# Post-norm transformer layer: transposing the softmax numerators with DMA in float16 halves, in a new order of work

## The chip, the cores and the metric

One core of one Trainium2 chip runs the whole layer in one launch. The metric is the device time of that launch in microseconds (us). The kernel before takes 672.68 us, the median of three runs (672.47 to 676.06).

## The reference

Four independent sequences of T=512 tokens with D=512 features go through one layer. All inputs and outputs are float32.

```python
q = (x @ Wq + bq)                 # 16 heads of 32
k = (x @ Wk + bk); v = (x @ Wv + bv)      # one key/value head shared by all 16
q, k = rotary(q), rotary(k)
attn = softmax(q k^T / sqrt(32))          # per head 512 x 512
x = layernorm(x + (attn v) @ Wo + bo)
quant(w) = clip(round(w / (mean|w| + 1e-8)), -1, 1)
hidden = sigmoid(x @ quant(w1)^T) * (x @ quant(w2)^T)    # 1408 wide
x = layernorm(x + hidden @ quant(w3)^T)
```

## The kernel before, in words

Five engines work at once, each from its own queue in order: TensorE (PE) multiplies, VectorE (DVE) and ScalarE (ACT) do elementwise work, GpSimd (POOL) helps and issues DMAs, SyncE (SP) issues DMAs. Order across engines is kept by counting semaphores: `wait_ge(sem, n)` in a queue blocks everything behind it in that queue until the count is reached.

**Periods.** `period(0)` does the attention of sequence 0 (`first_heads`) while the weights are loaded and rounded to -1, 0, 1. `period(b)`, b = 1 to 3, does the attention of sequence b, and beside it everything that comes after attention for sequence b-1: output projection (`project_out`), layer norm, transposing the normalised rows (`turn_h`), the up projections (`up`, two per tile f: one for the gate, one for the value), `down`. A tail does the rest of sequence 3.

**A head** is four score tiles of 128 queries x 512 keys (`score`, L1017). For each tile DVE takes the row maximum (`row_max`, L756), ACT the exponential with its row sum (`exps`, L526; an ACTIVATE and a READ_ACCUMULATOR) into p_sb. PE then transposes p in 128x128 blocks (`turn`, L1028), 16 a head, into two PSUM banks t_ps; ACT (`move`, L534) and DVE (`move`, L763) copy two of the four banks of a head each to pt_sb. After four heads `context` (L1084) multiplies pt_sb with v in float32: 16 products of 32 columns, four of them side by side in the array. `turn_sums`, `norm_row` and `normalise` divide by the row sums.

**What sets the order.** Each engine has a written order (`heads` for PE at L1138, ACT at L574, DVE at L812). BESIDE (L51) names the one late job that stands beside each head: head 0 to 3 up0 to up3, head 4 projection q2, and so on: at most one up tile a head. Between two periods stands a stage without heads (L1185 to L1202): q0, k, v, four output projections, four `turn_h`, q1. The score tiles go round three banks s_ps (four in sequence 0). a_ps and b_ps are filled by one job at a time; `up` fills a_ps with the gate and b_ps with the value; ACT takes tanh of a_ps (L509), DVE multiplies (`gate`, L707), ACT rounds the product to float16 (`g_high`, L518), DVE takes the remainder (`g_low`, L712). In ACT's order the `g_high` that is owed from the head before stands ahead of the exponentials.

**q** is rotated, split in two parts (hi, lo) and stacked for the scores by 16 DMAs of 64 KB per group of four heads (`stack`, L310): group 0 by SP, groups 1 to 3 by POOL. The rotation's cosine product is POOL's (L393), the sine product and the sum DVE's (L658, L667), in sequence 0 POOL's.

Of the kernel before, what the change touches and what calls it, by code (L numbers as in the profile page):

```python
# [20 lines left out]
F32 = mybir.dt.float32  # L22
F32R = mybir.dt.float32r
F16 = mybir.dt.float16
ALU = mybir.AluOpType
# [3 lines left out]
P = 128  # L29
# [6 lines left out]
FT = F // P  # L36
SCALE = float(HD) ** -0.5
# [4 lines left out]
G_SCALE = 2 * H_SCALE  # L42
PTR = HPG
QR = 2
SUMS = 4
PIECES = 4
SR = 3
# [3 lines left out]
BESIDE = (["up0", "up1", "up2", "up3", "q2", "up4", "up5", "up6", "q3"]  # L51
          + [f"up{f}" for f in range(7, FT)] + ["dn0", "dn1", "dn2", "dn3"])
FIRST_Q_AT = [3, 7]
DOWN_FIRST = 4
DOWN_CUT = 7


# [6 lines left out]
TAIL = [f"{stage}{t}" for stage in ("wo", "ht") for t in range(TT)]  # L64
LAST_CUT = 6


def is_tail(period):

    return isinstance(period, int) and period == B  # L70


def is_last(period):
    return isinstance(period, int) and period == B - 1


def norm_count(c, ln, t):


    n = (c * 2 + ln) * TT + t  # L80
    if isinstance(c, int) and (c, ln, t) == (B - 2, 1, TT - 1):
        n += TT
    elif isinstance(c, int) and (c, ln) == (B - 1, 0):
        n -= 1
    return n + 1


def late_bank(period, use):

    return "a" if use in ("wo0", "wo2", "wo3") else "b"  # L90


def bank_uses(bank, period):


    first = isinstance(period, int) and period == 0
    last = is_tail(period)
    uses = []
    if not last:
        uses += ["q0"] if bank == "a" else ["k"]  # L100
    if not first and not last:
        uses += [use for use in [f"{stage}{t}" for stage in ("wo", "ht") for t in range(TT)]
                 if late_bank(period, use) == bank]
    if not last and bank == "a":
        uses += ["q1"]
    for h in range(H + 1):
        use = BESIDE[h]
        if use[:1] == "q" and bank == "a" and not last:
            uses.append(use)
        elif use[:2] == "up" and not first:  # L110
            uses.append(use)
        elif use[:2] == "dn" and not first and (int(use[2:]) % 2 == 0) == (bank == "a"):
            uses.append(use)
        if h % HPG == 0 and h and bank == "a" and not last:
            uses.append(f"r{h // HPG - 1}")
    return uses


def at_use(bank, period, use):

    count = bank_uses(bank, period).index(use) + 1
    if isinstance(period, int) and period == 0:
        return count
    return len(bank_uses(bank, 0)) + (period - 1) * len(bank_uses(bank, None)) + count


def layer(nc, xT, x, wq, small, wo, b_rows, w1, w2, w3, table, out):
    with ExitStack() as ctx:
# [5 lines left out]

# [62 lines left out]

# [24 lines left out]
        b_drained = sem("b_drained")  # L222
        kv_filled = sem("kv_filled")
# [7 lines left out]
        q_in = [sem(f"q_in{j}") for j in range(HPG)]  # L231
        q_by_pool = [sem(f"q_by_pool{j}") for j in range(HPG)]
# [5 lines left out]
        pt_dve = sem("pt_dve")  # L238
        recip_done = sem("recip_done")
# [21 lines left out]

        def ain(b, use):

            return at_use("a", b, use)

        def bin_(b, use):
            return at_use("b", b, use)

        def wide(n):

            return (a_ps, a_filled, a_drained, ain) if n % 2 == 0 else (b_ps, b_filled, b_drained, bin_)

        def late_tile(b, use):

            if is_tail(b):
                ps = (s_ps + t_ps + [c_ps] + s_ps)[TAIL.index(use)]
                return ps, tail_filled, tail_drained, lambda b, use: TAIL.index(use) + 1
            return wide(0) if late_bank(b, use) == "a" else wide(1)

        def score_ring(b):  # L280

            return SR + 1 if isinstance(b, int) and b == 0 else SR

        def score_bank(b, n):
            return (s_ps + [b_ps])[n % score_ring(b)][:, :]

        def gated_tile(b, f):


            return raw[:, f % 2, :] if is_tail(b) else b_ps[:, :]  # L290

        def stacked(b, g, j):

            if isinstance(b, int) and b == 0:
                return q_in[j], (g + 1) * 16 * 4
            if g == 0:
                return q_in[j], (b + HG) * 16 * 4
            return q_by_pool[j], ((b - 1) * (HG - 1) + g) * 16 * 4

        def stack(engine, b, g):  # L300

            engine.wait_ge(hi_done, b * len(UNITS) + UNITS.index(f"q{g}") + 1)
            stand(engine)
            for j in range(HPG):
                for r in (0, 2, 1, 3):
                    half = (hi, lo)[r % 2]
                    if j == 0 and r == 1:
                        engine.wait_ge(lo_done, b * len(UNITS) + UNITS.index(f"q{g}") + 1)
                        stand(engine)
                    engine.dma_start(q_st[HD * r:HD * (r + 1), g % QR * HPG + j, :].bitcast(F32),  # L310
                                     half[HD * j:HD * (j + 1), :].bitcast(F32)).then_inc(stacked(b, g, j)[0], 16)
# [7 lines left out]


        @block.sync
        def _(sp):
            def load_xT(b):
                for half in range(2):
                    cols = slice(half * DT * T // 2, (half + 1) * DT * T // 2)
                    sp.dma_start(xT_sb[:, :, :].rearrange("p k t -> p (k t)")[:, cols],
                                 xT[b, :, cols]).then_inc(xT_in[half], 16)

            def store(c, t):
                sp.wait_ge(normed, norm_count(c, 1, t))  # L330
                stand(sp)
                sp.dma_start(out[c, t * P:(t + 1) * P, :], h_sb[:, t, :]).then_inc(h_free, 16)

            def period(b):
                first, last = isinstance(b, int) and b == 0, isinstance(b, int) and b == B - 1
                if first:
                    sp.wait_ge(xT_in[1], 16)
                    sp.dma_start(wq_sb[:, :, P:], wq[:, P:].rearrange("(k p) n -> p k n", p=P)).then_inc(wq_in, 16)
# [938 lines left out]
```

## Time and profile before

| | |
|---|---|
| median of three runs | 672.68 us |
| the profiled execution: its own time | 671.8 us |
| its span, first to last instruction | 670.0 us |
| granted TensorE clock, mean over the span | 0.983 |
| PE busy | 627.5 us (94%) |
| DVE busy | 458.3 us (68%) |
| ACT busy | 353.3 us (53%) |
| POOL busy | 202.1 us (30%) |

A busy share is the union of the engine's instructions. The durations of single instructions overlap their neighbours on the same engine a little, so a train of them takes less than the sum: the distance from one start to the next is what one costs the engine, its duration is what a dependent has to wait.

### The profile page before, as it was taken

Reading aid. Unit: us, or ns where it says so; the run is one execution under the profiler, and the core shown is the slowest. Engines: PE = TensorE matmul, PEld = TensorE weight load, DVE = VectorE, ACT = ScalarE, POOL = GpSimd, SP = SyncE. Lnnn points to the kernel's source line nnn. Section 1 sums busy time; section 2 is a strip of 40 time slices with the busy share of each in tenths; the row PEclk is TensorE's granted clock in tenths of the full one; section 3 lists DMA queues with packets and bytes.
Section 4 is the critical chain, followed back from the end, with each engine's and each line's share of the span. In section 5 each row is a group of like instructions: output and inputs, shape, how many; then the busy total and the mean of one; then the engine's idle time right before and its main releaser. Section 6 shows DMA issues by size and latency. Waiting matters only on the chain.

```text
span 670.0 us, 10715 instructions
## 1 busy us (share of the span) xinstructions
PE 627.5 (94%) x3342; PEld 340.9 (51%) x3342; DVE 458.3 (68%) x791; ACT 353.3 (53%) x814; POOL 202.1 (30%) x292
## 2 busy tenths in 40 slices
PE   5777968899999999999999999999999999999996
PEld 2544554345556556435656565534556564543442
DVE  2776777387878776577877785577878785655333
ACT  2787696316767675114867674313767675302320
POOL 1229689221450700121440610122422340110001
PEclk9699979999999999999999999999999999999999
DMA  7661532021221200022210400022201110000001
GB/s 275 216 232 32 204 94 98 0 64 64 64 64 55 73 1 1 35 84 75 65 44 21 127 1 1 33 79 80 63 21 44 32 33 0 28 22 16 1 1 63
DMA packets 18204, 41.93 MB, mean 63 GB/s; under 512 B 4704, under 2 KB 5856, under 8 KB 17632
## 3 DMA queue, kind: packets, MB, share of 16 engines
q1 hardware_dynamic: 12576, 30.42, 13.7%
q0 software_dynamic: 4608, 9.45, 5.8%
q10 hardware_dynamic: 960, 1.33, 0.5%
q8 instruction: 30, 0.49, 0.3%
q14 instruction: 30, 0.25, 0.1%
HBM read 20.20 MB, written 4.19 MB: 36 GB/s over the span
## 4 chain that ended last, share of the span: by engine, by line
PE 81%; DVE 5%; ACT 5%; issue 3%; DMA 3%; SPq 1%; POOL 0%; DVEq 0%; POOLq 0%; ACTq 0%
PE t_ps L1028 15%; PE b_ps L988 11%; PE a_ps L988 11%; PE c_ps L1084 9%; PE a_ps L942 8%; PE s_ps L1017 7%; PE a_ps L1003 6%; PE b_ps L1003 5%; PE a_ps L966 5%; DMA late<-in_w 2%; PE b_ps L966 2%; ACT p_sb L526 2%; SPq L310 1%; ACT pt_sb L534 1%; DVE sh_sb L756 1%
## 5 line engine op out<-in xcount | busy, mean ns | idle before, releaser
L526 ACT ACTIVATE p_sb<-s_ps,sh_sb 128x512 f32<-128x512 f32 x240 | 164.4, 689 | 87.1 <-DVE sh_sb L756 87.0
L756 DVE TENSOR_REDUCE sh_sb<-s_ps 128x1 f32<-128x512 f32 x240 | 157.9, 681 | 4.3 <-PE s_ps L1017 4.3
L1028 PE MATMUL t_ps<-table_sb,p_sb 128*128 128x128 f32 x1024 | 140.7, 280 | 13.4 <-ACT pt_sb L534 10.9
L1028 PEld LDWEIGHTS t_ps<-table_sb,p_sb 128*128 128x128 f32 x1024 | 120.2, 144 | 58.4 <-ACT p_sb L526 23.1
L763 DVE COPY pt_sb<-t_ps 128x512 f32<-128x512 f32 x128 | 88.3, 690 | 85.0 <-PE t_ps L1028 83.6
L534 ACT ACTIVATE pt_sb<-t_ps 128x512 f32<-128x512 f32 x128 | 76.5, 598 | 54.7 <-PE t_ps L1028 53.1
L1017 PE MATMUL s_ps<-k_st,q_st 128*128 128x512 f32 x240 | 89.9, 457 | 3.8 <-DVE k_st L676 2.0
L988 PE MATMUL b_ps<-late,q 128*128 128x512 f16 x352 | 83.5, 380 | 0.0
L988 PE MATMUL a_ps<-late,q 128*128 128x512 f16 x344 | 81.6, 380 | 2.0 <-DVE late L692 2.0
L417 POOL TENSOR_SCALAR rstd<-mv 128x1 f32<-128x1 f32 x32 | 8.5, 265 | 236.3 <-DVE mv L719 236.2
L393 POOL TENSOR_TENSOR rot<-raw,table_sb 128x512 f32<-128x512 f32 x20 | 25.4, 1272 | 154.7 <-ACT raw L493 139.3
L942 PE MATMUL a_ps<-xT_sb,wq_sb 128*128 128x512 f32 x128 | 62.3, 618 | 7.9 <-DMA wq_sb<-in_wq 6.8
L1084 PE MATMUL c_ps<-pt_sb,v_sb 128*32 128x512 f32 x512 | 60.5, 597 | 3.1 <-ACT pt_sb L534 3.1
L310 POOL DMA_DIRECT2D q_st<-hi x72 | 36.1, 506 | 59.2 <-DVE hi L683 51.8
L988 PEld LDWEIGHTS a_ps<-late,q 128*128 128x128 f16 x344 | 31.0, 98 | 43.5 <-issue 6.6
L988 PEld LDWEIGHTS b_ps<-late,q 128*128 128x128 f16 x352 | 31.8, 98 | 39.1 <-issue 5.3
L1017 PEld LDWEIGHTS s_ps<-k_st,q_st 128*128 128x128 f32 x240 | 42.3, 196 | 15.3 <-ACT p_sb L526 7.6
L526 ACT ACTIVATION_READ_ACCUMULATOR p_sb<-s_ps,sh_sb 128x1 f32 x240 | 48.2, 201 | 0.0
L1003 PE MATMUL b_ps<-q,late 128*128 128x512 f16 x176 | 41.3, 379 | 0.0
L1003 PE MATMUL a_ps<-q,late 128*128 128x512 f16 x176 | 40.4, 380 | 0.0
L942 PEld LDWEIGHTS a_ps<-xT_sb,wq_sb 128*128 128x128 f32 x128 | 23.6, 197 | 31.0 <-issue 20.7
L707 DVE SCALAR_TENSOR_TENSOR b_ps<-th,b_ps 128x512 f32<-128x512 f32 x33 | 23.0, 696 | 21.4 <-PE b_ps L988 19.1
(97 smaller groups left out, 679.1 us busy)
## 6 DMA issues: line engine op xcount, KB each, us to landing
late<-in_w SPq DMA_DIRECT2D x2, 2816.0 KB, 11.4
q_st<-hi POOLq DMA_DIRECT2D x72, 64.0 KB, 2.0
q_st<-lo POOLq DMA_DIRECT2D x72, 64.0 KB, 2.0
xT_sb<-in_xT SPq DMA_DIRECT2D x8, 512.0 KB, 4.7
late<-in_x SPq DMA_DIRECT2D x4, 1024.0 KB, 5.3
out<-late SPq DMA_DIRECT2D x16, 256.0 KB, 2.0
q_st<-hi SPq DMA_DIRECT2D x56, 64.0 KB, 2.0
q_st<-lo SPq DMA_DIRECT2D x56, 64.0 KB, 2.0
```

Source lines behind the costliest of these rows:

```text
L310: engine.dma_start(q_st[HD * r:HD * (r + 1), g % QR * HPG + j, :].bitcast(F32), half[HD * j:HD * (j + 1), :].bitcast(F32)).then_inc(stacke ...
L526: act.activation(p_sb[:, h % 2, t, :], score_bank(b, n), ACT.Exp, bias=sh_sb[:, n % (2 * SR):n % (2 * SR) + 1], scale=-1.0, accum_out=sums ...
L534: act.activation(pt_sb[:, h % PTR, k, :], t_ps[k % 2][:, :], ACT.Copy).then_inc(pt_act, 1)
L756: dve.tensor_reduce(sh_sb[:, n % (2 * SR):n % (2 * SR) + 1], score_bank(b, n), AX.X, ALU.min).then_inc(maxed, 1)
L763: dve.tensor_copy(pt_sb[:, h % PTR, k, :], t_ps[k % 2][:, :]).then_inc(pt_dve, 1)
L942: mm = pe.matmul(a_ps[:, :], wq_sb[:, k, g * P:(g + 1) * P], xT_sb[:, k, :], start=(k == 0), stop=(k == DT - 1))
L966: mm = pe.matmul(ps[:, :], cx[:, g, t * P:(t + 1) * P], wo_sb[:, g, :], start=(g == 0), stop=(g == HG - 1))
L988: mm = pe.matmul(ps[:, :], w[:, k, f * P:(f + 1) * P], hT[:, s, k, :], start=(k == 0 and s == 0), stop=(k == DT - 1 and s == 1))
L1003: mm = pe.matmul(ps[:, :], gT[:, s, f, t * P:(t + 1) * P], q3v[:, f, :], start=(f == 0 and s == 0), stop=(f == FT - 1 and s == 1))
L1017: pe.matmul(score_bank(b, n), q_st[:, h % (QR * HPG), t * P:(t + 1) * P], k_st[:, :], start=True, stop=True).then_inc(scored, 1)
L1028: mm = pe.transpose(t_ps[k % 2][:, t * P:(t + 1) * P], p_sb[:, h % 2, t, k * P:(k + 1) * P], id_sb)
L1084: mm = pe.matmul(c_ps[HD * j:HD * (j + 1), :], v_sb[:, k, :], pt_sb[:, (g * HPG + j) % PTR, k, :], start=(k == 0), stop=(k == TT - 1))
```

## The change

Sequence 0 stays nearly as it was. From sequence 1 on:

- Scores, maxima and buffers go by pairs of tiles: four PSUM banks hold two pairs, one maximum instruction reads a pair. The second transpose bank is now e_ps, a third bank for other jobs.
- p of a pair is scaled by 4096 and split: ACT writes the float16 rounding (`p_high`), DVE the float16 remainder (`p_low`). SP issues one DMA transpose of both halves, 512 KB, into pt_sb (`turn`), two a head. PE's 256 transposes a sequence and the 64 copies of `move` are gone.
- `context` multiplies both halves of p with both halves of v (v is scaled by a power of two and split, `values`, `value_halves`): 64 float16 products instead of 16 in float32, and it waits for the eight transposes of its group.
- There is no stage without heads: all jobs stand in BESIDE beside the 32 half heads, up to two up tiles a head in heads 6, 7, 10 and 11. The context of a group stands at the second head after it.
- All stacking is POOL's, head by head, and so is the rest of the rotation of q1 to q3 in every sequence. Loops over b are written out.

```diff
+BESIDE = [                       # (after the head's 1st pair of scores), (after its 2nd pair)
+    ([("dn2", -2)], []),
+    ([("sums3", -1), ("ctx3", -1)], [("dn3", -2)]),
+    ([("vp", 0), ("wo0", -1)], [("wo1", -1)]),
+    ([("wo2", -1)], [("wo3", -1), ("vs", 0)]),
+    ([("q2", 0)], [("vb", 0), ("ht0", -1), ("ht1", -1)]),
+    ([("ht2", -1), ("ht3", -1), ("ctx0", 0), ("sums0", 0)], [("up0", -1)]),
+    ([("up1", -1)], [("up2", -1)]),
+    ([("up3", -1)], [("up4", -1)]),
+    ([("q3", 0)], [("up5", -1)]),
+    ([("ctx1", 0), ("sums1", 0)], [("up6", -1)]),
+    ([("up7", -1)], [("up8", -1)]),
+    ([("up9", -1)], [("up10", -1)]),
+    ([("dn0", -1)], []),
+    ([("ctx2", 0), ("sums2", 0)], [("q0", 1)]),
+    ([("dn1", -1)], [("kp", 1)]),
+    ([("ks", 1)], [("q1", 1)]),
+]
+# PE
+            def heads(b):
+                for h in range(H):
+                    for half in range(2):
+                        score(b, h, half)
+                        for name, s in beside(b, h, half):
+                            use(name, s)
+            def score(b, h, i):
+                n = h * PAIRS + i
+                pe.wait_ge(expd, b * H * TT + max(2 * n - 2, 0))
...
+            def context(b, g):
+                pe.wait_ge(ctx_done, b * HG + g)
+                pe.wait_ge(v_lo, b)
+                for n in range(PSLOTS):
+                    pe.wait_ge(turned[n], ...)
+                for k in range(TT):
+                    for n in range(2):
+                        for m in range(2):
+                            for j in range(HPG):
+                                mm = pe.matmul(c_ps[HD * j:HD * (j + 1), :], vh[:, m, k, :],
+                                               pt_half[:, j, :, n, :, k, :], ...)
+# SP
+            def turn(b, h, i):
+                n = pair_of(b, h, i) % PSLOTS
+                sp.wait_ge(p_lo, pair_of(b, h, i) + 1)
+                sp.wait_ge(ctx_filled, b * HG + h // HPG)
+                sp.dma_start_transpose(pt_half[...], p_half[n][...]).then_inc(turned[n], 16)
+# ACT
+            def heads(b):
+                    exps(b, h, 0)
+                    exps(b, h, 1)
+                    if owed:
+                        g_high(owed[1], owed[0])
+                    for f, s in early:
+                        tanh(s, f)
+                    if h == 5:
+                        h_high(b - 1, 2)
+                        h_high(b - 1, 3)
+                    p_high(b, h, 0)
+                    for f, s in early:
+                        g_high(s, f)
...
+                    exps(b, h, 2)
+                    exps(b, h, 3)
...
+                    if h == 8:
+                        unit(b, "q3")
+                    if h % HPG == 1 and h > HPG:
+                        norm_row(b, h // HPG - 1)
+                    for f, s in late_ups:
+                        tanh(s, f)
+                        owed = f, s
+                    p_high(b, h, 1)
...
+# DVE
+            def heads(b):
+                    row_max(b, h, 0)
+                    if owed is not None:
+                        g_low(s, owed)
+                    if h:
+                        p_low(b, h - 1, 1)
...
+                    for f in early:
+                        gate(s, f)
+                    row_max(b, h, 1)
+                    for f in early:
+                        g_low(s, f)
+                    p_low(b, h, 0)
+                    if h == 5:
+                        h_low(s, 2)
+                        h_low(s, 3)
+                    for f in late_ups:
+                        gate(s, f)
+                        owed = f
...
```

`early` are the up tiles of the head's first half, `late_ups` those of its second. On DVE the output projections' sums, norms and `ffn_out` (the residual after `down`) stand between `p_low(b, h-1, 1)` and the early `gate`, or at the end of the head; in head 5 `norm(3)`, `h_low(0)` and `h_low(1)` stand ahead of the second maximum. A job waits until its bank's job before has been read: `ht0` and `ht2` share b_ps, `q3` and `up5` a_ps, `sums1` and `up6` a_ps, `dn2` and `sums3` a_ps.

## Rows read from the trace of the kernel before

**Rows 1.** Windows: sequence 0, periods 1 to 3, tail; PE, PEld, DVE, ACT, POOL busy, clock, DMA
```profile
0.00:128.70 128.70, 97.06 (x529) 56.78 (x529) 82.79 (x141) 85.92 (x197) 70.59 (x57) 0.92 0.44 150
128.70:282.50 153.80, 152.56 (x834) 83.51 (x834) 112.31 (x194) 83.90 (x197) 41.02 (x71) 1.00 0.17 46
436.00:587.10 151.10, 149.96 (x826) 82.44 (x824) 113.19 (x196) 83.92 (x197) 41.81 (x73) 1.00 0.16 43
587.10:670.00 82.90, 75.43 (x326) 34.38 (x322) 37.10 (x64) 15.66 (x26) 7.28 (x18) 0.99 0.05 19
```

**Rows 2.** The page's chain that ended last, by engine
```profile
PE 81%; DVE 5%; ACT 5%; issue 3%; DMA 3%; SPq 1%; POOL 0%; DVEq 0%; POOLq 0%; ACTq 0%
```

**Rows 3.** Groups by line and shape: count, busy us, mean ns of one, idle before
```profile
L1028 PE MATMUL t_ps<-table_sb,p_sb 128*128 128x128 f32 x1024 | 140.7, 280 | 13.4 <-ACT pt_sb L534 10.9 <-ACT p_sb L526 1.8
L763 DVE COPY pt_sb<-t_ps 128x512 f32<-128x512 f32 x128 | 88.3, 690 | 85.0 <-PE t_ps L1028 83.6
L534 ACT ACTIVATE pt_sb<-t_ps 128x512 f32<-128x512 f32 x128 | 76.5, 598 | 54.7 <-PE t_ps L1028 53.1
L756 DVE TENSOR_REDUCE sh_sb<-s_ps 128x1 f32<-128x512 f32 x240 | 157.9, 681 | 4.3 <-PE s_ps L1017 4.3
L724 DVE TENSOR_SCALAR late<-late,mv,rstd 128x512 f32<-128x512 f32 x32 | 17.2, 536 | 9.1 <-POOL rstd L420 9.0
L543 ACT ACTIVATE q<-late 128x1408 f16<-128x1408 f32 x12 | 16.5, 1383 | 1.5 <-DMA late<-in_w 1.3
L1057 PE MATMUL c_ps<-table_sb,rexp 128*128 128x32 f32 x32 | 3.9, 266 | 0.0
```

**Rows 4.** Timeline of PE, period 1: context, then one head with an up tile (start, us)
```profile
189.52 3.64 PE L1084 MATMUL c_ps<-pt_sb,v_sb 128*32 128x512 f32 x32
196.79 0.94 PE L1017 MATMUL s_ps<-k_st,q_st 128*128 128x512 f32 x3
197.57 1.90 PE L988 MATMUL a_ps<-late,q 128*128 128x512 f16 x8
199.31 1.04 PE L1028 MATMUL t_ps<-table_sb,p_sb 128*128 128x128 f32 x8
202.96 0.94 PE L1017 MATMUL s_ps<-k_st,q_st 128*128 128x512 f32 x3
```

**Rows 5.** Timeline of DVE and ACT in that head
```profile
198.87 1.28 DVE L756 TENSOR_REDUCE sh_sb<-s_ps 128x1 f32<-128x512 f32 x2
199.59 0.69 ACT L526 ACTIVATE p_sb<-s_ps,sh_sb 128x512 f32<-128x512 f32 x1 [0.42 <-DVE sh_sb L756]
200.27 0.68 ACT L526 ACTIVATE p_sb<-s_ps,sh_sb 128x512 f32<-128x512 f32 x1
200.93 0.59 ACT L534 ACTIVATE pt_sb<-t_ps 128x512 f32<-128x512 f32 x1
201.41 0.60 ACT L509 ACTIVATE th<-a_ps 128x512 f32<-128x512 f32 x1
```

**Rows 6.** Timeline of heads of sequence 0 that have no other work beside them
```profile
113.16 1.16 PE L1028 MATMUL t_ps<-table_sb,p_sb 128*128 128x128 f32 x8 [0.34 <-ACT pt_sb L534]
...
117.88 1.16 PE L1028 MATMUL t_ps<-table_sb,p_sb 128*128 128x128 f32 x8 [0.34 <-ACT pt_sb L534]
```

**Rows 7.** DMA issues (KB each, median us to landing)
```profile
late<-in_w SPq DMA_DIRECT2D x2, 2816.0 KB, 11.4
q_st<-lo POOLq DMA_DIRECT2D x72, 64.0 KB, 2.0
```

**Rows 8.** Windows of sequence 0 at the lower clock (columns as in the first group)
```profile
24.00:28.00 4.00, 4.00 (x12) 2.50 (x11) 2.28 (x5) 4.00 (x9) 2.55 (x2) 0.50 0.59 133
88.00:92.00 4.00, 2.45 (x10) 2.38 (x11) 2.74 (x5) 4.00 (x13) 3.83 (x4) 0.50 0.33 80
```

More of the change, by code:

```diff
@@ L42 @@
 G_SCALE = 2 * H_SCALE
+P_SCALE = 2.0 ** 12
+V_TOP = 14
+EXPONENT = 0x7F800000
 PTR = HPG
-QR = 2
+PSLOTS = 4
+QR = 5
 SUMS = 4
 PIECES = 4
-SR = 3
+FIRST_RING = 4
 UNITS = ["q0", "k", "q1", "q2", "q3"]
[L51 to L55, printed above, removed]
+FIRST_Q_AT = [3, 7, 15]
+FIRST_Q = [(0, 2), (0, 3), (1, 0)]
 ABS_AT = [0, 0, 1, 1, 2, 3, 4, 5, 9, 9, 10, 10]
@@ L61 @@
 ROUND = 1.5 * 2.0 ** 23
[L64 to L90, printed above, removed]
@@ L93, in bank_uses @@
[L93 to L116, printed above, removed]
@@ new lines, with beside @@
+LAST_BESIDE = {13: ([("ctx2", 0), ("sums2", 0)], [("dn1", -1)]), 14: ([("dn2", -1)], []), 15: ([], [])}
+TAIL = ([("dn3", B - 2), ("sums3", B - 1)] + [(f"ht{t}", B - 1) for t in range(TT)]
+        + [(f"up{f}", B - 1) for f in range(FT)] + [(f"dn{t}", B - 1) for t in range(TT)])
+def beside(b, h, half):
+    uses = BESIDE[h][half]
+    if b == B - 1 and h in LAST_BESIDE:
+        uses = LAST_BESIDE[h][half]
+    return [(use, b + of) for use, of in uses if not (use[:2] == "dn" and b + of < 0)
+            and not (b == 1 and (use, of) in (("sums3", -1), ("ctx3", -1)))]
@@ L284, in score_bank @@
[L284 to L311, printed above, removed]
+        wide = {"a": (a_ps, a_filled, a_drained), "b": (b_ps, b_filled, b_drained),
+                "e": (e_ps, e_filled, e_drained)}
@@ L375, in _ @@
+            turn(B - 1, H - 1, 1)
+            for t in range(1, TT):
+                store(B - 2, t)
             for t in range(TT):
                 store(B - 1, t)
-            sp.wait_ge(h_free, (B + 1) * TT * 16)
+            for t in range(TT):
+                sp.wait_ge(h_free[t], (B + 1) * 16)
         @block.gpsimd
@@ L910, in _ @@
+            first_heads()
+            rotate(1, "q0")
+            halves(1, "q0")
+            normalise(0, HG - 1)
+            pairs(1, "k")
+            rotate(1, "k")
+            halves(1, "k")
+            for b in range(1, B):
+                heads(b)
+            p_low(B - 1, H - 1, 1)
+            reciprocals(B - 1, HG - 1)
+            norm(B - 2, 1, 2)
+            ffn_out(B - 2, 3)
+            norm(B - 2, 1, 3)
+            normalise(B - 1, HG - 1)
             for t in range(TT):
+                attended(B - 1, t)
```

1367 lines of the change are left out of this document (730 added, 637 removed).

## The prediction, made before the changed kernel was built or run

> **What bounds the kernel now.** I read the windows first: in the three periods PE is busy 152.6 of 153.8 us and 150.0 of 151.1, DVE about 113, ACT 84 [rows 1]. The chain of waits agrees: 81% of it is PE [rows 2]. So a microsecond taken from PE in a period is a microsecond off the kernel, but only until another engine, or the order of the queues, stops it. The bound is near: DVE has 40 us of room a period. Sequence 0 (128.7 us) is different: PE is busy 97 us there, and what sets its pace is the ring score, maximum, exponential, transpose.
>
> **What PE loses and gains.** From one head's scores to the next are 202.96 - 196.79 = 6.17 us; eight float16 products take 199.31 - 197.57 = 1.74 us, 0.2175 each [rows 4]. Sixteen of them (3.48) and the scores (0.94) leave 1.75 us for 16 transposes, 28 us a sequence. The context is the term that the trace does not show. Now it is 32 instructions in 3.64 us, four column groups side by side, so 8 rounds of 0.45 [rows 4]. The float16 one is 64 products, 16 rounds. Lower end: 16 x 0.2175 = 3.5 us. Upper end: each pair of weight load and product costs what the small products of L1057 cost, 3.9 / 32 = 0.12 us [rows 3], 64 x 0.12 = 7.7. I take 3.6, because the context's own row is the nearest and it does overlap. PE's work per sequence then falls from 152.5 to about 124.5 us.
>
> **What ACT and DVE lose and gain.** I distinguish the distance between starts (what an instruction costs its engine) from its duration (what the next engine waits). On ACT exponentials start 0.67 us apart, a copy costs 0.48; on DVE two maxima take 1.28, so one costs 0.60 and lasts 0.68 [rows 5].
> - ACT drops 32 copies a sequence (15 us) and gets 32 `p_high` of 1024 columns. From 598 ns at 512 columns and 1383 at 1408 [rows 3] another 512 columns are 0.45 us: 0.93 each, 29 us. ACT: 84 to 98 us.
> - DVE drops 32 copies (19 us). A maximum over a pair is 0.60 + 0.53 = 1.13 us (a 512-column pass is 0.536 [rows 3]), 32 x 1.13 = 36 for 64 x 0.60 = 38. `p_low` reads two operands of 1024 columns: by the same sum 1.13, 36 us a sequence. Bounds: half of that if the wide form runs faster (18), and 1.30 each when POOL's work slows it. Rotation moved to POOL gives back 4, the bound and halves of v cost 1.5. DVE: 113 to about 125 us.
> - POOL gets 16 more stacking DMAs and six more rotation products a sequence, some 53 us of work in a period; SP has 32 transposes to issue, and `load_x` waits behind the turn of head 5, `add_bias` behind that, two stacks behind `add_bias`. In the timetable below none of them is waited for, since q is stacked two to four heads ahead. They cost nothing as long as heads last over 8 us.
>
> If only these sums counted, the change would pay: see the first rival. But every engine works strictly in its written order, and the new order puts dependent work on three engines into one ring.
>
> **The ring of a head with two up tiles** (heads 6, 7, 10, 11). Pass a semaphore in 0.05 us, and start when DVE begins the first maximum: maximum 1.30; two exponentials on ACT 1.34 (0.67 each); the owed `g_high`, which now stands behind them, 0.67; DVE, which has stood at `g_low` all that time, does it in 0.60; `p_low` of the head before 1.13; early `gate` 0.60; second maximum 1.30; two exponentials 1.34; late tanh 0.67; late `gate` 0.60; next head. Sum 9.55 us. PE has only 0.94 + 4 x 1.74 = 7.9 us to do in it, so PE waits. Before, the same two tiles stood beside two heads of 6.17.
>
> **The other heads** I carried through in the same way: each instruction starts when the one before it in its queue has left the engine and all that it waits for is done. The method can be tried on sequence 0, where a ring and not PE sets the pace: it gives 4.69 us for a plain head, and the trace has 117.88 - 113.16 = 4.72 [rows 6]. For sequence 2, heads 0 to 15, it gives
> 13.3, 13.0, 9.2, 8.3, 10.8, 18.7, 9.5, 9.6, 14.2, 14.4, 9.6, 9.6, 11.8, 12.2, 10.6, 12.7: 187 us, where the period now takes 153.5. The long ones are these.
> - Head 0: `dn2` (22 x 0.2175 = 4.8 us) stands on PE ahead of the second pair of scores; DVE idles 6.9 us for it. Head 1: `sums3` waits until DVE has read `dn2`'s bank, then the context (3.6) stands ahead of the second scores.
> - Head 5: `ht2` waits for `h_low(0)` of the same bank, which stands behind a maximum, `p_low` and a norm; then the context; the second scores come 5.1 us late. Then `up0` waits for `h_low(3)`, and `gate` for `up0`: 3.9 us.
> - Heads 8 and 9: `up5` needs a_ps, which holds q3 until ACT reads it behind the second exponentials; DVE stands at `gate` meanwhile, 4.8 us. Head 9 is the same with the row sums (`norm_row`).
> - Head 15 and the next 0: k of the next sequence is rotated and split only when its scores are next.
>
> **The sum.** Sequence 0 to the first maximum of sequence 1: 128.7 [rows 1] and about ten dependent steps of 0.7 for k (its product, bias, rotation, halves, score), 136 us. Sequence 1 has no late `dn`, `sums3` and `ctx3` in heads 0 and 1: 170. Sequence 2: 187. Sequence 3, whose last heads have little beside them, to its last exponential: 177. Tail on PE from there: output projections and `dn3` not yet done 12, context 3.6, last group 3.4; then 6.5 for sum, statistics, norm, transpose, halves; up 11 x 3.48 = 38.3; down 4 x 4.79 = 19.2; last norm and store 6: 89 (now 82.9 [rows 1]). Together 136 + 534 + 89 = 759 us of span. The profiled execution is 1.8 us above its span now and the median 0.9 above that: **762 us**, 13% slower. (A difference under 0.5% could not be told from none here.)
>
> **Transfers.** The trace has no transpose by DMA. Lower end: the large weight loads move 2816 KB in 11.4 us [rows 7], so 512 KB in 2.1. Upper end: eight times a small transfer of 64 KB, issue to landing 2.0 [rows 7], 16 us. I take 3, plus 2 to land, since a 512 KB transfer is nearest to the large loads. In the timetable nothing changes up to 4.5 us per transfer; 5 gives 554 in place of 534, 6 gives 626, 8 gives 810.
> The Trainium skill's VectorE: DVE Perf Modes, section The three transpose paths, prices a 128x128 transpose in 2-byte numbers at 1309 ns by DMA; a transfer here has 16 such blocks, which would be an estimated 21 us, far slower than TensorE. Its DMA: Bandwidth & Descriptors, section Latency and other measured facts, has 261 GB/s for such transposes, an estimated 2.0 us a transfer, which by the timetable would be hidden. No row here decides between them.
>
> **The clock.** Where PE worked with gaps in sequence 0 the granted clock fell to 0.50, the lower level of 1.2 GHz, for instance in 88 to 92 with PE busy 2.45 of 4 us [rows 8]; in the periods it is 1.00 [rows 1]. After the change PE is busy some 65% of a period. If the mean were 0.92 as in sequence 0, PE's 124.5 us would grow by 11 a sequence, partly on the ring: bounds 0 and +33, taken as 0, since mostly PE is what waits.
>
> **Rivals.**
> 1. The queues overlap better than the timetable has it, and the fullest engine sets the pace: DVE's 125 us a sequence. 136 + 375 + 89 + 2.7 = 603 us. For it: PE is at 99% now, its order is loose enough. Against: the ring of 9.55 us is dependent work, and sequence 0, also a ring, has no engine above 76% [rows 1]. It decides if heads 6 and 7 last under 7.9 us. This is the other side. 0.13.
> 2. The ring holds, but the long heads do not: all 16 heads take about 9.6. 136 + 3 x 153 + 89 + 2.7 = 687 us. 0.10.
> 3. The DMA transposes bound it: every transfer above 4.5 us is waited for by the exponentials (four buffers) and the contexts. At 6 us each 762 + 92 = 854 us, at 8 us 1038; at the upper end of 16 us the 96 transfers alone would take 1536, the whole 1764. For it: no row shows such a transfer. Against: nothing but the rate of the large loads. 0.15. (The 1309 ns of the skill's page VectorE: DVE Perf Modes would put it beyond that upper end.)
> 4. As forecast, 0.62. Its own range: `p_low` at half -25, context at 7.7 us +37, DVE at 1.30 +9, clock up to +33: 735 to 815.
>
> **Range and chances.** The range takes in rival 2 and rival 3 up to 6 us: 685 to 860; outside remain rival 1 and the slow half of rival 3, about 0.2. Faster by over 0.5%: rival 1 and a sliver of 2, 0.14. Within 0.5% lies none of the cases, 0.02. Slower: 0.84.
>
> **What would show it.** In the profile after, heads 6, 7, 10, 11 start 9.6 us apart and head 5 is the longest; DVE's `g_low` begins after an idle 2 us that ended with ACT's `g_high`; `gate` in heads 8 and 9 after more than 4; PE is busy under 75% in a sequence with a mean clock below 0.98; the contexts last 3.6 us and don't end on a DMA wait; `p_low` starts 1.13 before the next instruction. I am wrong if PE or DVE is above 90% busy in a sequence, or if exponentials idle on transfers.

## The result and the profile after

The changed kernel takes **829.68 us** (median), the kernel before 672.93 beside it: a ratio of 1.227, 95% interval 1.217 to 1.238. One of its four executions took 1060.36 us at a clock of 0.55 and is left out of the comparison. The forecast of 762 had the sign right and was 68 us short. The time lies in the whole range, 685 to 860, but above the 735 to 815 that the forecast gave its own case: the part of the range that it fell into had been allowed for slow transfers, which did not happen.

The page of the changed kernel: span, busy time by engine, the granted clock in 40 slices, the chain that ended last, and the main groups.

```profile
span 827.4 us, 9098 instructions
PE 608.9 (74%) x2964; PEld 288.1 (35%) x2964; DVE 510.7 (62%) x698; ACT 394.4 (48%) x814; POOL 256.4 (31%) x358
PEclk9899898969889886897988989679888898987998
PE 41%; DVE 28%; ACT 12%; issue 12%; DMA 4%; SPq 2%; POOL 0%; DVEq 0%; ACTq 0%; POOLq 0%
L621 ACT ACTIVATE p_all<-s_ps,sh_sb 128x512 f32<-128x512 f32 x192 | 130.0, 682 | 240.2 <-DVE sh_sb L883 240.1
L883 DVE TENSOR_REDUCE sh_sb<-s_ps 128x2 f32<-128x1024 f32 x96 | 116.8, 1218 | 93.2 <-PE s_ps L1201 93.2
L890 DVE SCALAR_TENSOR_TENSOR p_all<-p_all 128x1024 f16<-128x1024 f32 x96 | 131.6, 1371 | 3.6 <-ACT p_all L629 3.5
L629 ACT ACTIVATE p_all<-p_all 128x1024 f16<-128x1024 f32 x96 | 101.7, 1059 | 1.4
L1253 PE MATMUL c_ps<-pt_sb,vh 128*32 128x512 f16 x768 | 59.3, 478 | 11.9 <-DMA pt_sb<-p_all 11.9
```

No engine is full. PE was 81% of the chain [rows 2] and is 41% now; maxima, exponentials and scores wait for each other (L621 for L883, L883 for L1201). The window of sequence 2, then the waits of DVE and PE (us, times, longest):

```profile
323.60:531.80 208.20, 146.49 (x708) 66.44 (x708) 131.04 (x166) 97.66 (x197) 59.56 (x96) 0.84 0.61 117
```
```profile
DVE late L842 <- ACT late L600: 49.3, 32, 2.0
DVE b_ps L837 <- PE b_ps L1163: 47.1, 12, 6.1
DVE e_ps L837 <- PE e_ps L1163: 28.2, 8, 7.1
...
PE b_ps L1138 <- DVE late L828: 29.0, 3, 9.7
PE a_ps L1221 <- DVE late L860: 12.2, 2, 6.1
PE c_ps L1253 <- DMA pt_sb<-p_all: 11.9, 3, 4.0
PE s_ps L1201 <- DVE k_st L785: 10.8, 3, 4.8
```

A period of 151 to 154 us at clock 1.00 [rows 1] is now, in sequence 2, 208 at 0.84. Of the 32 waits of `g_low` for `g_high` (L842 for L600), 21 last 2.00 us, seven in each sequence from head 6 to head 12: they are the ring of the prediction. The other 11, of 0.66 us, are the tail's. The ring's length can be read from the maxima of heads 10 and 11 (DVE timeline; the first maximum of a head is the one behind the late `gate`):

```profile
462.95 1.22 DVE L883 TENSOR_REDUCE sh_sb<-s_ps 128x2 f32<-128x1024 f32 x1
...
472.40 1.22 DVE L883 TENSOR_REDUCE sh_sb<-s_ps 128x2 f32<-128x1024 f32 x1
...
481.85 1.22 DVE L883 TENSOR_REDUCE sh_sb<-s_ps 128x2 f32<-128x1024 f32 x1
```

9.45 us, twice; the prediction said 9.55. All heads of sequence 2, read in the same way (us from a head's first maximum to the next head's); the last line is of experiment e12 below:

| head | 0 | 1 | 2 | 3 | 4 | 5 | 6 | 7 | 8 | 9 | 10 | 11 | 12 | 13 | 14 | 15 | sum |
|---|---|---|---|---|---|---|---|---|---|---|---|---|---|---|---|---|---|
| forecast | 13.3 | 13.0 | 9.2 | 8.3 | 10.8 | 18.7 | 9.5 | 9.6 | 14.2 | 14.4 | 9.6 | 9.6 | 11.8 | 12.2 | 10.6 | 12.7 | 187 |
| measured | 15.3 | 15.1 | 9.4 | 8.3 | 12.6 | 23.4 | 13.8 | 9.4 | 16.3 | 15.6 | 9.4 | 9.5 | 7.9 | 17.9 | 10.7 | 13.5 | 208 |
| e12 | 13.4 | 13.3 | 9.4 | 8.3 | 12.6 | 20.6 | 9.4 | 9.4 | 13.9 | 17.1 | 9.9 | 9.5 | 7.9 | 15.5 | 10.7 | 13.4 | 194 |

**Where the 68 us lie.** First maximum of sequence 1 at 133.8 (forecast 136); the sequences take 189.8, 208.2 and 194.5 (170, 187, 177), the third up to the last exponential, and the tail after it 101.1 (89).

### The profile page after: what moved, and what is told of

It is laid out like the page before. It is cut to its first block, busy times and chain, and to the rows that moved or that the text cites. A ratio compares the mean times of both kernels' runs of the same rounds, so it can differ in the third digit from the quotient of the medians.

```text
span 827.4 us, 9098 instructions
## 1 busy us (share of the span) xinstructions
PE 608.9 (74%) x2964; PEld 288.1 (35%) x2964; DVE 510.7 (62%) x698; ACT 394.4 (48%) x814; POOL 256.4 (31%) x358
## 4 chain that ended last, share of the span: by engine, by line
PE 41%; DVE 28%; ACT 12%; issue 12%; DMA 4%; SPq 2%; POOL 0%; DVEq 0%; ACTq 0%; POOLq 0%
DVE sh_sb L883 10%; DVE p_all L890 8%; PE a_ps L1163 6%; PE c_ps L1253 6%; ACT p_all L621 5%; PE b_ps L1175 3%; PE a_ps L1175 3%; PE b_ps L1163 3%; PE a_ps L1094 2%; PE a_ps L1148 2%; PE s_ps L1201 2%; PE c_ps L1239 2%; PE e_ps L1163 2%; PE s_ps L1148 2%; PE b_ps L1148 2%
## 5 line engine op out<-in xcount | busy, mean ns | idle before, releaser
L621 ACT ACTIVATE p_all<-s_ps,sh_sb 128x512 f32<-128x512 f32 x192 | 130.0, 682 | 240.2 <-DVE sh_sb L883 240.1
L883 DVE TENSOR_REDUCE sh_sb<-s_ps 128x2 f32<-128x1024 f32 x96 | 116.8, 1218 | 93.2 <-PE s_ps L1201 93.2
L1163 PE MATMUL a_ps<-late,q 128*128 128x512 f16 x352 | 103.8, 448 | 71.9 <-ACT th L592 29.6
L890 DVE SCALAR_TENSOR_TENSOR p_all<-p_all 128x1024 f16<-128x1024 f32 x96 | 131.6, 1371 | 3.6 <-ACT p_all L629 3.5
L629 ACT ACTIVATE p_all<-p_all 128x1024 f16<-128x1024 f32 x96 | 101.7, 1059 | 1.4
L1201 PE MATMUL s_ps<-k_st,q_st 128*128 128x512 f32 x192 | 80.8, 509 | 19.2 <-DVE k_st L785 10.8
L461 POOL TENSOR_TENSOR rot<-raw,table_sb 128x512 f32<-128x512 f32 x20 | 25.8, 1290 | 144.0 <-ACT raw L571 136.2
L1253 PE MATMUL c_ps<-pt_sb,vh 128*32 128x512 f16 x768 | 59.3, 478 | 11.9 <-DMA pt_sb<-p_all 11.9
L1201 PEld LDWEIGHTS s_ps<-k_st,q_st 128*128 128x128 f32 x192 | 35.8, 198 | 43.6 <-issue 24.5
L837 DVE SCALAR_TENSOR_TENSOR b_ps<-th,b_ps 128x512 f32<-128x512 f32 x24 | 16.7, 696 | 51.2 <-PE b_ps L1163 47.1
L369 POOL DMA_DIRECT2D q_st<-lo x96 | 47.3, 497 | 0.0
L1163 PE MATMUL b_ps<-late,q 128*128 128x512 f16 x192 | 46.5, 386 | 0.0
L592 ACT ACTIVATE th<-a_ps 128x512 f32<-128x512 f32 x44 | 26.3, 598 | 41.3 <-PE a_ps L1163 41.3
L842 DVE TENSOR_TENSOR late<-b_ps,late 128x512 f16<-128x512 f32 x24 | 16.6, 692 | 40.0 <-ACT late L600 40.0
L608 ACT ACTIVATE p_all<-s_ps,sh_sb 128x512 f32<-128x512 f32 x48 | 32.9, 692 | 15.9 <-DVE sh_sb L877 15.9
L1163 PE MATMUL e_ps<-late,q 128*128 128x512 f16 x160 | 40.3, 397 | 0.0
```

Source lines behind the costliest of these rows:

```text
L369: engine.dma_start(q_st[HD * r:HD * (r + 1), slot, :].bitcast(F32), half[HD * (h % HPG):HD * (h % HPG + 1), :].bitcast(F32)).then_inc(stac ...
L608: act.activation(p_sb[:, h % 2, t, :], first_bank(n), ACT.Exp, bias=sh_sb[:, n % (2 * PSLOTS):n % (2 * PSLOTS) + 1], scale=-1.0, accum_out ...
L621: act.activation(p_pair[n][:, t % 2, :], pair_banks(h * PAIRS + t // 2)[:, t % 2, :], ACT.Exp, bias=sh_sb[:, 2 * n + t % 2:2 * n + t % 2 + ...
L629: act.activation(p_half[n][:, 0, :], p_pair[n].rearrange("p t k -> p (t k)"), ACT.Copy, scale=P_SCALE).then_inc(p_hi, 1)
L883: dve.tensor_reduce(sh_sb[:, 2 * n:2 * n + 2], pair_banks(h * PAIRS + i), AX.X, ALU.min).then_inc(maxed, 2)
L890: dve.scalar_tensor_tensor(out=p_half[n][:, 1, :], in0=p_pair[n].rearrange("p t k -> p (t k)"), scalar=P_SCALE, in1=p_half[n][:, 0, :], op ...
```

## What two timelines show

PE in head 5 of sequence 2:

```profile
377.55 0.70 PE L1201 MATMUL s_ps<-k_st,q_st 128*128 128x512 f32 x2
387.91 1.09 PE L1138 MATMUL b_ps<-table_sb,late 128*128 128x128 f32 x4 [9.66 <-DVE late L828]
388.79 1.06 PE L1138 MATMUL e_ps<-table_sb,late 128*128 128x128 f32 x4
389.79 5.56 PE L1253 MATMUL c_ps<-pt_sb,vh 128*32 128x512 f16 x64
...
400.21 3.27 PE L1163 MATMUL a_ps<-late,q 128*128 128x512 f16 x8 [3.81 <-DVE late L828]
```
```profile
388.00:393.00 5.00, 5.00 (x40) 2.71 (x44) 0.36 (x1) 2.14 (x3) 0.00 (x0) 0.50 0.00 0
```

PE waits 9.7 us for `h_low(0)` (L828). After that wait the granted clock is 0.50, the 1.2 GHz level, and the context takes 5.56 us in place of the 3.64 that it takes at full clock, as in head 8:

```profile
446.45 3.64 PE L1253 MATMUL c_ps<-pt_sb,vh 128*32 128x512 f16 x64
```

Eight products last 3.27 in place of 1.89. This work is on the path: the second scores stand behind it.

POOL and DVE in head 6:

```profile
411.16 4.94 POOL L492 TENSOR_TENSOR late<-late,b_sb 128x512 f32<-128x512 f32 x4
411.64 5.55 DVE L890 SCALAR_TENSOR_TENSOR p_all<-p_all 128x1024 f16<-128x1024 f32 x1
```

One `p_low` of 32 in each sequence lasts 5.55 us in place of 1.22: it begins 0.5 us after the first of POOL's four bias additions has begun and ends about 1 us after the last one has ended. Head 6 is 13.8 us long for it, not 9.5.

## The experiments

Each is the changed kernel with the edit shown. Times are medians; the kernel before took 673 to 675 us beside them.

**e1: the owed `g_high` first.** On ACT:

```diff
+                    if owed:
+                        g_high(owed[1], owed[0])
+                        owed = None
                     exps(b, h, 0)
                     exps(b, h, 1)
-                    if owed:
-                        g_high(owed[1], owed[0])
-                        owed = None
```

> Edit: in ScalarE's order the owed g_high stands ahead of the first two exponentials of a head, nothing else. If the ring of dependent work in the heads with two up tiles sets the pace, those heads fall from 9.5 to about 7.8 us and heads 8, 9 and 12 by 1 to 2 each; the timetable then has the three sequences at 511 in place of 536 us, so about 804 us for the kernel (changed kernel 829.7). If the transposes by DMA are the bound (4.85 us each back to back, eight of them between two contexts), heads 9 and 13 wait longer for them and most of it is given back: 820 or more. If TensorE's lower clock is all that is wrong, nothing changes but for the clock.

Measured: 785.5 us, ratio 1.164 (1.158 to 1.170), 44 us under the changed kernel where 25 were expected. Its wait, against 49.3 us above:

```profile
DVE late L842 <- ACT late L600: 7.3, 11, 0.7
```

What is left are the 11 waits of the tail; the 21 of 2.00 us are gone. Heads 7, 10 and 11 last 7.8 to 8.0 us, about PE's own work (7.9 in the forecast). The ring was real and one misplaced instruction closed it. Part of the extra gain is in head 6 (13.8 to 9.9) and head 13 (17.9 to 15.9). In head 6 the long `p_low` starts later within POOL's four additions and again ends about 1 us behind the last of them: it lasts 3.76 us, not 5.55.

**e2: reads of a_ps first.** On ACT `unit(b, "q3")` (head 8) and `norm_row` (heads 5, 9, 13) move from behind to ahead of the second exponentials:

```diff
+                    if h == 8:
+                        unit(b, "q3")
+                    if h % HPG == 1 and h > HPG:
+                        norm_row(b, h // HPG - 1)
                     exps(b, h, 2)
                     exps(b, h, 3)
...
-                    if h == 8:
-                        unit(b, "q3")
-                    if h % HPG == 1 and h > HPG:
-                        norm_row(b, h // HPG - 1)
```

> Edit: ScalarE reads q3 (head 8) and the turned row sums (heads 5, 9, 13) ahead of the second pair of exponentials of the head, nothing else. If the bank a_ps is what up5, up6 and q0 wait for, heads 8 and 9 fall from 16.3 and 15.6 us to about 11 to 12, VectorE's idle time at gate there goes, and the kernel takes about 802 us. If the transposes bind, context 2 waits for them by as much more (4.0 us now, then up to 12) and the kernel stays above 815. If the clock is the cause, TensorE's gap in heads 8 and 9 closes and the granted clock rises from 0.868.

Measured: 791.3 us, ratio 1.171 (1.164 to 1.177), 38 us less. `gate`'s waits for `up` fall from 47.1 and 28.2 us to

```profile
DVE b_ps L837 <- PE b_ps L1163: 33.6, 13, 6.6
DVE e_ps L837 <- PE e_ps L1163: 7.0, 5, 1.4
```

Heads 8, 9 and 13 last 10.9, 10.6 and 13.3 us (16.3, 15.6, 17.9). So a bank's late read does hold up the next job of that bank. The waits of 5.5 to 6.6 us that are left are those of head 5 and the first of the tail.

**e3: POOL's additions spread.** One addition between two stackings in place of four in a row:

```diff
-                add_bias(b)
                 stack(pool, b, 10)
+                add_bias(b, [0])
                 stack(pool, b, 11)
+                add_bias(b, [1])
...
```

> Edit: GpSimd adds the output bias to the four tiles of x one at a time between its stacking DMAs, not four in a row (4.94 us). One p_low in each sequence lasted 5.55 us in place of 1.22 and ended with GpSimd's fourth addition. If GpSimd's float32 additions keep VectorE's p_low from finishing, the longest p_low is then below 2.6 us, head 6 falls from 13.8 to about 9.5 to 11, and the kernel takes 816 to 822 us. If that instruction was long for another reason (its data, a semaphore), nothing changes: 829.

Measured: 812.4 us, ratio 1.205 (1.202 to 1.208), 17 us less: 5.8 a sequence, more than the 4.3 of the long `p_low`. In sequence 2 head 6 falls from 13.8 to 9.4 us, and head 13 from 17.9 to 15.6. `p_low` now (min, median, max in ns):

```profile
L895 DVE SCALAR_TENSOR_TENSOR p_all<-p_all x96: 1207/1215/1719, 137.8 to 710.4; 128x1024 f16<-128x1024 f32 x96
```

Its longest is 1.72 us. So it was POOL's four additions in a row that made one `p_low` 4.3 us longer. The Trainium skill's SBUF — State Buffer, section SBUF: two separate sides, says that DVE and GpSimd share a pair of ports as an exclusive lock: of a DVE instruction with two SBUF inputs and a GpSimd one that reads SBUF, the one that starts first keeps it for its whole instruction. The trace agrees and goes further: `p_low` was held up not for one addition (1.27 us) but until the fourth had ended.

**e4: transfers of 256 KB.** Only the high half of p is transposed and the context reads it twice; the low half of p is left out.

```diff
                 sp.dma_start_transpose(
-                    pt_half[:, h % PTR, i, :, :, :, :].rearrange("p s t k q -> p (s t k) q"),
-                    p_half[n][:, :, :].rearrange("p s c -> p (s c)")).then_inc(turned[n], 16)
+                    pt_half[:, h % PTR, i, 0, :, :, :].rearrange("p t k q -> p (t k) q"),
+                    p_half[n][:, 0, :]).then_inc(turned[n], 16)
```

> Edit: each DMA transposes only the high half of p, 256 KB; the context reads that half twice, so the instructions of all engines stay the same in number and shape (the low half of p is left out of the output). If the transposes are behind the ring, only context 2's waits of 4.0 us go: 829.7 - 3 x 4 = 818 us, perhaps 5 less by the clock. If the transposes are the bound (as in the rival of the prediction), back to back they take 2.4 in place of 4.85 us and the kernel falls by far more, below 760. If a transpose is mostly fixed cost, 7 in a row still take over 30 us and nothing changes.

Measured: 819.3 us, ratio 1.214 (1.211 to 1.218), 10 us less: the 818 of "behind the ring", far from the 760 that transfers as the bound would have given. Median from issue to landing, changed kernel and this one:

```profile
pt_sb<-p_all SPq DMA_TRANSPOSE x96, 4.6
```
```profile
pt_sb<-p_all SPq DMA_TRANSPOSE x96, 3.1
```

**e5: PE kept busy.** Products that nobody reads, in c_ps while it is free, in the places where PE stood still:

```diff
+FILL = {(0, 0, "dn2"): (18, 3, 1), (1, 0, "sums3"): (24, 3, 1), (5, 0, "ht2"): (42, 0, 0),
+        (8, 1, "up5"): (22, 1, 0), (13, 0, "ctx2"): (14, 2, 0)}
...
+                for _ in range(n):
+                    pe.matmul(c_ps[:, :], q1v[:, 0, 0:P], q1v[:, 0, 0:512], start=True, stop=True)
```

> The changed kernel with products added on PE whose result nobody reads: 18 before dn2 in head 0, 24 before sums3 in head 1, 42 before ht2 in head 5, 22 before up5 in head 8, 14 before ctx2 in head 13, each group about as long as the idle time that the changed kernel's trace has there (4.5, 6.1, 9.7, 5.4, 4.0 us). Nothing else moves. Theory (part of what was missed is the clock: after each long wait PE works at 0.50 for some us and the queue behind it is late): the contexts, which take 5.0 to 6.0 us behind such a wait, take 3.64, eight products 1.74 in place of 3.3 to 3.6, head 5 falls from 23.4 to about 19, heads 0, 1, 9 and 13 by 1 to 2 each; mean clock from 0.87 to 0.95, time 829.7 - 3 x 8 = about 805 us. Rival (the waits are set by ACT and DVE whatever PE's clock is, so it costs nothing): 829.7 or, since the added products stand in PE's queue, up to 10 us more.

Measured: 804.0 us, ratio 1.194 (1.191 to 1.197): **PE does 318 products more and the kernel is 26 us faster.** Mean clock 0.921 in place of 0.868. Head 5 again, with the last 19 of its 42 added products and the context at 3.64 us:

```profile
373.74 4.26 PE L1251 MATMUL c_ps<-q 128*128 128x512 f16 x19
378.59 0.63 PE L1138 MATMUL b_ps<-table_sb,late 128*128 128x128 f32 x4 [0.59 <-DVE late L828]
379.06 0.60 PE L1138 MATMUL e_ps<-table_sb,late 128*128 128x128 f32 x4
379.59 3.64 PE L1262 MATMUL c_ps<-pt_sb,vh 128*32 128x512 f16 x64
...
388.08 3.57 PE L1163 MATMUL a_ps<-late,q 128*128 128x512 f16 x8 [3.81 <-DVE late L828]
```

All 12 contexts now take 3.64 us. Heads 0, 1, 5, 8 and 13 fall by 1.8, 1.8, 2.8, 2.4 and 2.3 us; head 9 grows by 1.0. The products at 388.08 are still slow: ahead of them PE waits 3.8 us while c_ps is in use, and nothing was added there. So 26 us is what this experiment got back, and not all that the clock cost.

**e12: e5 and e3 together**, the two terms that the forecast took at nothing:

> The changed kernel with the two terms taken away that the forecast had at nothing, and its order as it is: the added products on PE (alone 829.7 - 25.7 = 804) and POOL's four bias additions spread (alone 829.7 - 17.3 = 812.4). If they are separate they add up: 829.7 - 43 = 787 us, with a mean clock above 0.92 and heads 6 at 9.5; 25 us above the forecast of 762. If both had removed the same time: about 804.

Measured: 791.6 us, ratio 1.172 (1.168 to 1.176), 38 of the expected 43 us. They are two causes; 5 us are common to both.

**e6: the edits of e1, e2 and e3 together.**

> The changed kernel with the three edits of order together: the owed g_high ahead of the exponentials, q3's and the row sums' reads on ACT ahead of the second exponentials, POOL's four bias additions spread between stackings. Alone they gave -44, -38 and -17 us. If they simply add: 730 us. Theory (a transfer of 512 KB takes about 4.85 us when they queue, and the turns of a group of heads can't start before the context before it has ended, so 8 x 4.85 = 39 us lie between two contexts): contexts 1 and 2 now wait on transfers in each sequence, and 15 to 27 us of the gain are given back: 745 to 757 us, with PE's waits for the transfers above 20 us in all. Slower than the kernel before in either case by over 8%.

**e7: e6 with the transfers of e4** (low half of p left out):

> As the run with the three edits of order, but a transfer turns only the high half of p (256 KB), and the context reads it twice, so that the products stay as many; the low half of p is left out of the result. With 3.1 us to landing and at most about 2.5 us each in a queue, transfers bind nothing: 715 to 735 us, 20 to 27 us under the run with whole transfers. If transfers were not what the three edits run into, it is within 5 us of that run.

**e8: e6 with the added products of e5:**

> The three edits of order and the added products of the clock experiment together. Where the order is better PE waits less, so the clock is already higher: some 0.90 without the added products. Theory: another 10 to 25 us under the run with the three edits alone, about 730 us; still slower than the kernel before (674.5). If the clock is free, as the forecast took it: no gain, up to 8 us more.

Measured: e6 748.1 us, ratio 1.110 (1.107 to 1.113); e7 741.3, 1.100 (1.098 to 1.103); e8 741.3, 1.100 (1.096 to 1.103). e6 came where it was expected, for a reason that holds only in small part. It gives back 18 of the 100 us that its edits gave alone, but halving the transfers (e7) brings only 7 of them; 20 to 27 were expected. PE was expected to wait over 20 us for transfers, and ACT's exponentials not at all. In e6:

```profile
PE c_ps L1258 <- DMA pt_sb<-p_all: 5.1, 3, 2.2
ACT p_all L626 <- DMA pt_sb<-p_all: 10.6, 5, 3.6
```

In e7 PE's are 2.7 us in all and ACT has none. Most of the rest is gain counted twice: e1 and e3 both cured head 6 (-3.9 and -4.4 us alone, -5.6 together) and, with e2, head 13. The transfers were not queued at 4.85 us each: I had read the pace of the ring, two turns in 9.45 us, as the pace of the transfers. One that nothing stands ahead of shows it, the second turn of head 11 in the changed kernel (DVE's `p_low`, then PE's context):

```profile
485.68 1.22 DVE L890 SCALAR_TENSOR_TENSOR p_all<-p_all 128x1024 f16<-128x1024 f32 x1
...
491.32 1.04 PE L1253 MATMUL c_ps<-pt_sb,vh 128*32 128x512 f16 x8 [3.97 <-DMA pt_sb<-p_all]
```

`p_low` ends at 486.90, the context starts 4.4 us later. That is one transfer's latency, and the wait is there because the ring made `p_low` late. From 397 to 404 us, where three transfers follow each other, the windows of 1 us have 197 to 218 GB/s: an estimated 2.4 to 2.7 us for the 524 KB of one.

e8 brought 7 us where 10 to 25 were expected, at a mean clock of 0.943 for 0.897. Its added products also cost time: head 8 lasts 13.0 us in each sequence, 9.3 in e6, since q3's bank is read early there: PE waits only 0.9 us ahead of `up5` in e6, and the 22 products put there take 4.75.

**e9: e6 with another order on PE.**

```diff
-    ([("dn2", -2)], []),
-    ([("sums3", -1), ("ctx3", -1)], [("dn3", -2)]),
+    ([], [("dn2", -2)]),
+    ([("ctx3", -1)], [("sums3", -1), ("dn3", -2)]),
...
-    ([("ht2", -1), ("ht3", -1), ("ctx0", 0), ("sums0", 0)], [("up0", -1)]),
+    ([("ctx0", 0), ("ht2", -1), ("ht3", -1)], [("sums0", 0), ("up0", -1)]),
```

> The three edits of order and, beside them, a new order on PE in three heads: dn2 behind the second scores of head 0 in place of ahead of them, sums3 behind the second scores of head 1, and in head 5 the context ahead of ht2 and ht3 (so that PE works while it would wait for h_low) and sums0 behind the second scores. Nothing is added or left out. Theory (the long heads are waits of the written order, and PE has the time for all of it): by the timetable of the prediction head 0 goes from 13.3 to 10.0, head 1 from 13.0 to 9.7, head 5 from 18.7 to 14.7, 25 us in all: 748 - 25 = 723, down to 713 where the clock falls less often. Rival (the transfers or DVE hold the heads together, and a wait only moves on): within 8 us of 748. Still slower than the kernel before (673) by 6 to 8%.

Measured: 714.5 us, ratio 1.057 (1.053 to 1.061), 34 us under e6 with the same work. Heads 0, 1 and 5 last 12.5, 9.9 and 18.7 us (15.2, 15.1, 23.4 in e6). In head 5 the context now waits for the halves of v:

```profile
341.91 4.46 PE L1258 MATMUL c_ps<-pt_sb,vh 128*32 128x512 f16 x40 [5.44 <-DVE vh L827]
```

**e11: e6 with p as one float16 number.** The transfers of e4, no `p_low`, 32 products in a context. The low half of p is left out.

```diff
-                sp.wait_ge(p_lo, pair_of(b, h, i) + 1)
+                sp.wait_ge(p_hi, pair_of(b, h, i) + 1)
...
-                    for n in range(2):
+                    for n in range(1):
```

> The three edits of order, and p is used as one float16 number: p_low is left out on DVE, the transfer turns only the high half (256 KB), the context has 32 products in place of 64. The low half of p is left out of the result. It asks what the second half costs. By the timetable with p_low at 0, the context at 1.8 us and a transfer at 1.3 plus 1.8: 441 us for the three sequences in place of 474, so 748 - 33 - 2 = 713 us (705 to 725). If p_low and the transfers lie beside other work, it is 741 or more, like the run with half transfers. In neither case under the kernel before (673): then what makes it slower is the order of the queues and not the float16 split.

Measured: 703.5 us, ratio 1.042 (1.038 to 1.045). The second half of p costs 45 us; 35 were expected, 23 to 43 by the range. But even without it this order of the queues loses to the kernel before, and e9 with both halves is only 11 us behind it: the second half and the order of three heads (34 us, e9) cost about as much.

**e13: e9 and e11 together, and the exponential writes float16 itself.** Beside the edit shown, `p_high` is gone, k is read earlier in head 15, and the halves of v are made ahead of q2's rotation.

```diff
-                act.activation(p_pair[n][:, t % 2, :], pair_banks(h * PAIRS + t // 2)[:, t % 2, :], ACT.Exp,
+                act.activation(p_half[n][:, 0, (t % 2) * T:(t % 2 + 1) * T],
+                               pair_banks(h * PAIRS + t // 2)[:, t % 2, :], ACT.Exp,
...
-                sp.wait_ge(p_hi, pair_of(b, h, i) + 1)
+                sp.wait_ge(expd, (b * H + h) * TT + (i + 1) * 2)
```

> All that the runs pointed to in one kernel: the three edits of order, the new order on PE in heads 0, 1 and 5, and p as one float16 number that the exponential writes itself. So p_high (1.06 us, 32 a sequence on ACT) and p_low (1.22 us, 32 a sequence on DVE) are both gone, the transfer is 256 KB, the context 32 products; on ACT k's read comes ahead of the last pair of exponentials of head 15, on DVE the halves of v ahead of q2's pairs. The low half of p and the scale of 2^12 on its high half are left out. By the timetable the three sequences go from 441 us (one half, with p_high, measured 703.5 in all) to 401: 703.5 - 40 = 664 us, 655 to 672, that is 1 to 2 per cent under the kernel before (674); heads 0, 1, 5, 15 at about 9, 8, 12.5 and 8. If instead the transfers or the clock hold it, 680 or more.

Measured: **646.8 us**, ratio 0.961 (0.959 to 0.963): faster than both kernels, for p held to float16. Its page and sequence 2:

```profile
PE 541.1 (84%) x2580; PEld 266.5 (41%) x2580; DVE 386.0 (60%) x602; ACT 301.3 (47%) x718; POOL 251.5 (39%) x358
PE 59%; DVE 17%; ACT 9%; issue 8%; DMA 2%; SPq 1%; POOL 1%; DVEq 0%; ACTq 0%; POOLq 0%
```
```profile
264.80:407.20 142.40, 122.21 (x581) 59.07 (x580) 89.60 (x134) 66.62 (x165) 58.25 (x96) 0.95 0.56 113
```

A sequence takes 142 us, under the 151 to 154 of before [rows 1], and PE is busy 122 of them. Heads 6, 7, 10 and 11 last 7.8 us. Heads 0, 5 and 15 last 11.0, 13.8 and 10.7, each longer than expected (9, 12.5, 8). The gain over e11 is 57 us where 40 were expected; which of the edits brought it was not separated. The three sequences together are 407 us, near the timetable's 401; in e11 they are 465 for its 441.

## Why the prediction was right, and where it was short

- **The mechanism held.** PE's relief is not worth its time, since the queues' order closes a ring. Forecast 9.55 us, measured 9.45; `g_low` waits the 2 us that ended with `g_high` in all 21 places behind a late up tile; `gate` waits 7.1 and 6.0 us in heads 8 and 9, where 4.8 was forecast; head 5 is the longest. e1 and e2 take those waits away by order alone and get 44 and 38 us. Rival 1, 603 us, needed an order that this kernel has not: e9 shows that much is in it, 115 us under the changed kernel with the same work.
- **Luck.** That 829.7 lies in the stated range owes nothing to the forecast's own case, which was given up to 815 (the four terms listed for it, added up, would have given 841). The room above was meant for transfers of up to 6 us.
- **Prices that held.** Context 3.6 (3.64 at full clock; 8 of the 12 took 5.0 to 6.0, and all took 3.64 in e5, so that belongs to the clock below). ACT 98 us a sequence (97.7). `p_low` 1.13 between starts (1.22 long). Transfer 3 us, 5 to landing (an estimated 2.4 to 2.7, and 4.6 to landing); in the changed kernel the exponentials never wait for it, and rival 3 fell. The Trainium skill's DMA: Bandwidth & Descriptors, section Latency and other measured facts, gives 261 GB/s for DMA transposes; 197 to 218 were measured here. The Trainium skill's VectorE: DVE Perf Modes, section The three transpose paths, gives 1309 ns for one 128x128 block; 16 blocks in one transfer land in 4.6 us here, so it can't be scaled by blocks.
- **A sign that failed.** Contexts were not to end on a transfer; context 2 does, 4 us in each sequence. Head 12 came out at 7.9 us and not 11.8, so context 2 comes early; heads 12 and 13 together are 25.8 for 24.0. With half transfers (e4) the longest such wait is 2.8.
- **The clock, the term that was mis-sized.** "Bounds 0 and +33, taken as 0, since mostly PE is what waits". It cost 26 us by e5, inside those bounds. The reason given was wrong: PE waits, and then what it does behind the wait (`ht2`, the context, `up`) is what everyone waits for, at half the clock. PE's 124.5 us of work a sequence became 146.5 busy at a mean clock of 0.84 in sequence 2, 136.2 at 0.91 in e9. The rows of sequence 0 had shown the gaps and the clock [rows 8].
- **POOL, the second.** "They cost nothing", and `p_low` at most 1.30 beside POOL. It was 5.55 once a sequence, and in head 4 the halves of v (L820, L822) took 0.91 and 1.37 us beside POOL's rotation, where the forecast had 1.5 for the bound and all of the halves. In e13, where POOL does nothing at that moment, the same two take 0.29 and 0.35 us: POOL's part is 1.65 us a sequence. `p_low` lasts 1371 ns in the mean for a median of 1216. e3 puts the first part at 17 us. DVE's 125 us a sequence became 131.
- **The tail**: 12 us for the last output projections and `dn3` after the last exponential; they end 14.2 us behind it, a norm and the transpose to the first `up` take 9.8 for 6.5, and from the first `up` to the end are 68.5 for 63.5: 101 us for 89. Why was not taken apart.
- What remains once the clock and POOL's additions are out (e12, 791.6 for 762) is this tail (12 us) and, in sequence 2, heads 4, 5 and 9, 1.8 to 2.7 us each. In head 4 it is the halves of v. Heads 5 and 9 were not taken apart; in head 5 the products behind the second wait are still slow in e5's timeline, and head 9 is 1 us longer with the added products than without them.

## What to carry over

When a change unloads the engine that bounds a kernel, cost the queues' order before the engines' sums: write the ring of one head out instruction by instruction, and ask of every queue whether something that others wait for stands behind something that waits itself. After its waits of 9.7 and 3.8 us in head 5 PE worked at the lower clock; where such work is on the path, price it at that clock. And before a second pass over the data is paid for (the low half of p, 45 us here), ask whether the result needs it and whether the first form can be written where the number is made.

## What the hardware showed unexpectedly

- PE got 318 more products of 512 columns and the kernel was 26 us faster (e5): the granted clock stayed up where PE had stood still for 4.5 to 9.7 us.
- A DVE instruction with two operands in SBUF (1.22 us) lasted 5.55 us beside four float32 additions of POOL in a row (4.94 us), and 1.72 at most where the additions were spread (e3). Two small ones of 128x128 took 0.91 and 1.37 us beside POOL's rotation, 0.29 and 0.35 without (e13).
- A DMA transpose of 512 KB lands 4.6 us after its issue, one of 256 KB 3.1 (medians, changed kernel and e4); a line through the two is an estimated 1.6 us and 3.0 us per 512 KB.
- An exponential of 128x512 that writes float16 lasts as long as one that writes float32: 683 ns in e13, 682 in the changed kernel.
